# GpSimd normalises the next sequence's rows in place of VectorE, in a gated cross-attention and expert block

## The reference, cut to what matters

```python
def _layernorm(x, axis=-1, eps=1e-05):
    m = jnp.mean(x, axis=axis, keepdims=True)
    v = jnp.var(x, axis=axis, keepdims=True)
    return (x - m) / jnp.sqrt(v + eps)

# attention, 16 heads of 16 columns, causal over the 512 rows, on x = layernorm(x)
q, k, v = heads(x @ Wq + bq), heads(x @ Wk + bk), heads(x @ Wv + bv)
att = where(causal, q k^T / 4, -inf);  y = softmax(att) @ v
y = y + softmax(qc kc^T / 4) @ vc            # the same rows against the context
return y @ Wp + bp

x = x + tanh(g_xattn) * attention(layernorm(x), ctx)
x = x + tanh(g_ffn) * experts(layernorm(x))  # top 2 of 16, and a shared one with a convolution
```

## Times and profile before

| | us |
|---|---|
| median of 3 runs | 1772.03 |
| lowest and highest | 1766.85, 1774.86 |
| the profiled execution | 1767.04 |
| its span, from the first to the last instruction | 1765.3 |
| its mean granted TensorE clock, share of full speed | 0.967 |

### The profile page before, as it was taken

One profiled execution on the slowest core, in us unless ns is written; L12 is line 12 of the kernel. 1 busy time (PEld: TensorE's weight loads), 2 busy tenths in 40 slices (PEclk: granted clock), 3 DMA queues, 4 the chain that ended last, 5 costly groups with the idle time before them and its releaser, 6 DMA issues.

```text
span 1765.3 us, 36714 instructions
## 1 busy us (share of the span) xinstructions
PE 1588.7 (90%) x11515; PEld 958.3 (54%) x11515; DVE 1240.4 (70%) x3358; ACT 841.1 (48%) x1716; POOL 937.2 (53%) x1556
## 2 busy tenths in 40 slices
PE   2499899989999999999999999999975999997997
PEld 1245455545545554555555555555543999984554
DVE  1377677767777777777777777777844776665776
ACT  1156455555556555555655555555441444431111
POOL 3134455635445554544555454455544766647775
PEclk9799999999999999999999999999986999998999
DMA  3443656555544656565355655546444666656886
GB/s 105 133 130 94 136 99 161 95 143 120 138 122 101 163 96 159 110 142 130 93 165 101 151 125 127 136 87 164 95 128 113 183 172 172 171 149 194 258 259 196
DMA packets 215399, 247.95 MB, mean 140 GB/s; under 512 B 51368, under 2 KB 168624, under 8 KB 215216
## 3 DMA queue, kind: packets, MB, share of 16 engines
q1 hardware_dynamic: 177136, 191.06, 44.0%
q0 software_dynamic: 17344, 35.75, 7.9%
q10 hardware_dynamic: 20736, 18.88, 3.1%
HBM read 160.04 MB, written 85.53 MB: 139 GB/s over the span
## 4 chain that ended last, share of the span: by engine, by line
PE 66%; DVE 9%; POOL 7%; issue 6%; DMA 4%; ACT 3%; SPq 1%; DVEq 0%; POOLq 0%; ACTq 0%
PE pv_self L1256 9%; PE scalar_bank L1184 9%; PE scalar_bank L1195 8%; PE vector_bank L1668 7%; POOL pt L1789 6%; PE vector_bank L1230 6%; DVE nmax L1049 4%; PE vector_bank L1227 4%; PE vector_bank L1299 3%; PE vector_bank L1141 3%; PE pv_cross L1239 3%; PE vector_bank L1174 3%; PE pv_cross L1676 2%; PE scalar_bank L1657 2%; PE pv_self L1676 2%
## 5 line engine op out<-in xcount | busy, mean ns | idle before, releaser
L1049 DVE TENSOR_REDUCE nmax<-vector_bank 128x1 f32<-128x384 f32 (+4 forms) x832 | 513.4, 640 | 164.2 <-PE vector_bank L1230 158.1
L752 ACT ACTIVATE pt<-scalar_bank 128x512 f32<-128x512 f32 x640 | 363.2, 598 | 239.9 <-PE scalar_bank L1195 238.1
L615 POOL TENSOR_SCALAR_AFFINE_SELECT pt<-pt 128x256 f32<-128x256 f32 (+1 forms) x640 | 224.4, 366 | 151.1 <-ACT pt L752 142.6
L1195 PE MATMUL scalar_bank<-stack 99*64 99x512 bf16 (+4 forms) x1280 | 294.4, 321 | 3.2 <-DMA stack<-max_scratch 2.2
L627 POOL TENSOR_TENSOR parts<-q,parts 128x1600 bf16<-128x1600 f32 x32 | 103.1, 3222 | 289.1 <-ACT parts L728 289.1
L1230 PE MATMUL vector_bank<-stack 96*128 96x128 bf16 (+3 forms) x1024 | 249.0, 302 | 0.0
L1227 PE MATMUL vector_bank<-tri,ident_b 128*128 128x128 bf16 (+2 forms) x704 | 176.4, 251 | 49.6 <-DVE nmax L1049 17.5
L1184 PE MATMUL scalar_bank<-xnT,w_qk 128*128 128x512 f32 x384 | 194.6, 632 | 1.3 <-ACT xnT L705 1.3
L1227 PEld LDWEIGHTS vector_bank<-tri,ident_b 128*128 128x128 bf16 x704 | 68.5, 97 | 231.3 <-DVE nmax L1049 115.6
L1500 POOL DMA_INDIRECT pt<-xn_rows,idx x144 | 144.2, 1001 | 77.8 <-issue 62.0
L1256 PE MATMUL pv_self<-pt,vst 128*32 128x512 f32 (+3 forms) x2048 | 181.3, 443 | 3.2 <-ACT usum L739 2.0
(11 more groups left out here) (213 smaller groups left out, 2689.2 us busy)
## 6 DMA issues: line engine op xcount, KB each, us to landing
qk_scratch<-parts SPq DMA_DIRECT2D x32, 1200.0 KB
stack<-qk_scratch SPq DMA_DIRECT2D x128, 192.0 KB, 4.3
stack<-qk_scratch SPq DMA_DIRECT2D x256, 72.0 KB, 3.3
results<-pt ACTq DMA_DIRECT2D x144, 128.0 KB
stack<-qk_scratch SPq DMA_DIRECT2D x128, 128.0 KB, 4.1
stack<-qk_scratch SPq DMA_DIRECT2D x256, 36.0 KB, 3.0
xt<-in_x_dram SPq DMA_DIRECT2D x17, 512.0 KB, 4.2
xr<-in_x_dram SPq DMA_DIRECT2D x16, 512.0 KB, 5.0
```

The lines of the kernel that those rows point to most:

```text
L615: pool.affine_select(out=v, in_=v, compare_op=ALU.is_ge, fill=0.0, base=0, pattern=pat, channel_multiplier=-1).then_inc(masked, 1)
L752: act.activation(dst, bank(kind, ("st", c, k))[:, :], ACT.Exp, scale=SCALE).then_inc(scalar_drained, 1)
L1049: dve.tensor_reduce(dst, src, axis=AX, op=ALU.max, negate=True).then_inc(vector_drained, 1)
L1195: return pe.matmul(out, stack[c][0:rows, head, key0:key0 + nk], stack[c][0:rows, head, q0:q0 + nq], start=True, stop=True, **kw)
```

## The change

GpSimd does what `ln_apply` did for every sequence but the very first, whose four tiles stay on VectorE. In the bodies with a current and a next sequence one tile stands in each of the steps 8 to 11 of group (1, 1), ahead of the step's scatter and mask. In the prologue the four tiles stand in a row between `rstd` and `split_max`.

```diff
-LN_ROWS = {(1, 20 + t): t for t in range(4)}
+LN_ROWS = {8 + t: t for t in range(4)}
@@ gpsimd
+            def normalised(kind, b, t):
+
+                if t == 0:
+                    pool.wait_ge(rstd_ready, LN.upto(kind, b, 0) + 1)
+                    pool.wait_ge(scalar_filled, SU.upto(kind, b, ("xT", QT - 1)))
+                last = pool.tensor_scalar(xn[:, t, :], xt[:, t, :], mv[:, t, 0:1], rstd[:, t:t + 1],
+                                          ALU.subtract, ALU.mult)
+                if t == QT - 1:
+                    last.then_inc(xn_ready, 1)
+
             def mask_group(kind, b, c, g):
 
                 for k, name in enumerate(GROUP):
+                    if k in LN_ROWS and (c, g) == (1, 1) and PARTS[kind][2]:
+                        normalised(kind, b, LN_ROWS[k])
...
                 if nxt and not cur:
                     rstd_of(LN.upto(kind, b, 0) + 1)
+                    for t in range(QT):
+                        normalised(kind, b, t)
                     split_max(kind, b, 0, 0)
@@ vector, beside
-                    if (c, k) in LN_ROWS:
-                        if LN_ROWS[c, k] == 0:
-
-                            dve.wait_ge(scalar_filled, SU.upto(kind, b, ("xT", QT - 1)))
-                        ln_apply(n, LN_ROWS[c, k])
```

## The result

The changed kernel took 1843.47 us in the median of 4 runs (1836.64 to 1848.0), the kernel before 1770.33 beside it on the same chip: ratio 1.0408, 95% interval 1.0367 to 1.045. It is 73 us slower; 14 were forecast (1785.9), and 1843 lies outside the range of 1771 to 1803. The profiled execution took 1848.0 us, its span 1846.3; it is the longest of the four, as the profiled one before (1767.04) is near the shortest of its own, so that the two traces lie 81 us apart and not 73.

A forecast was written before the change was run, and what follows sets the result against it. TensorE was taken to bound the kernel, with GpSimd's masks already holding its products; 14 x 0.90 = 12.6 us plus 1.3 in the prologue gave 13.9, on the 1772.03 median 1785.9 us, range 1771 to 1803.

The forecast's parts named there:

- the price of the tile: One normalising tile on GpSimd, called c, was taken at 0.45 us, with ends of 0.40 and 0.82.
- The dearest value that I allowed: A GpSimd tile at twice VectorE's 486 ns, 0.97 us, giving 43.7 us of loss and 1815.7; chance 0.03.
- The rule of the queue: Last head group: products end later by the largest of 2c, 3c - 0.5 and 4c - 1.0, 0.90 us a sequence.
- A3: Mask of head 3's first key tile, last head group; two tiles ahead delay it 2c, forecast as deciding, 0.90 us.
- prologue 4.9 - 0.5: Prologue: TensorE gets the split maxima 4c later, forecast 1.8 us, less 0.5 given back by VectorE; net 1.3 us.
- The first sequence, counted at 0: Sequence without scatters: mask A3 has 2.0 us in hand and its masks wait for ScalarE, so no loss, 0.
- The freed VectorE: VectorE's freed 1.94 us a sequence counted as nothing; the rival that it wins gave 1756.8 us, chance 0.05.
- GpSimd takes up its lag before the additions into y: After the masks, GpSimd's extra lag of 4c fits in its 1.92 us idle before the additions, less TensorE's own 0.9.
- GpSimd is dearer: Rival: a tile costs 0.72 to 0.82 us and the last mask decides, 29 to 35 us lost; chance 0.16 overall.
- the marks that the text set for being wrong: Steady sequence near 76 us, idle at the products over 1.5 us, or low stretches in over ten or under four sequences.
- more of the low clock: Rival: all 14 steady sequences get a low-clock stretch, six more costing 10 us, 1796 us; chance 0.16.
- VectorE's tile beside it had stretched the mask B3 by 0.1 us: Last head group: this mask took 0.51 us where 0.40 is usual; without VectorE's overlap 0.1 us comes back.

The follow-up runs named there:

- forms: Changed kernel with each of the four GpSimd tiles in another form (one or two steps, column scalars or immediates); 1915.51 us against 1864.45 before, ratio 1.0282.
- copy4: Changed kernel with each GpSimd tile a plain copy of x in the same place; 1878.0 us against 1864.45 for the kernel before, ratio 1.0084.
- late1: Changed kernel with each GpSimd tile one mask later, the fourth behind all masks; 1898.46 us against 1859.32 for the kernel before, ratio 1.0216.
- moved: Changed kernel with the last head group's two scatters behind its last mask; 1789.82 us against 1761.66 for the kernel before, ratio 1.0164.
- after2: The changed kernel again, unaltered, on another chip; 1828.08 us against 1761.66 for the kernel before, ratio 1.0378.
- prologue: Changed kernel with only the prologue's four tiles on GpSimd, VectorE normalising in all bodies; 1862.74 us against 1859.32 for the kernel before, ratio 1.0024.
- free: Kernel before, VectorE leaving out the steady sequences' tiles but keeping their waits and signal, GpSimd untouched; 1757.7 us against 1761.66, ratio 0.9979.
- none: Changed kernel without the GpSimd tiles, their two waits left on GpSimd; 1872.58 us against 1864.45 for the kernel before, ratio 1.0041.
- before2: The kernel before once more, unchanged, for differences between chips; 1857.36 us against 1859.32, ratio 0.9998.

## Why the prediction was wrong

**The step that failed is the price of the tile**: "With the fixed part of the opcode and the slope of the one-input operation, 0.233 + 252 x 0.000875 = 0.45 us." It measured 1.22 us. A slope was carried from one opcode (the mask) to another because both read one tensor. forms and copy4 show that the number of inputs doesn't set it: with one input each, tensor_scalar took 848 to 1235 ns and the copy 395. The dearest value that I allowed, twice VectorE's time, 0.97 us, was still too low: the ratio to VectorE's mean of 486 ns is 2.5, and to its median of 414 it is 3.0. With that, also the weighing of ends failed: the row of the same opcode bounded only its fixed part, and no row bounded its slope from above.

The Trainium skill, "GPSIMD Engine Reference", section 4.1, has a one-input operation on GpSimd at about line rate. The copy fits that (395 ns, where VectorE's copies of this size, out of PSUM, took 412 to 417 in the kernel before), and the mask (409 ns) is near it; the normalising (1224 ns) and its plainest form (848 ns) do not fit. The opening of the page, VectorE roughly 2x faster, pointed the right way and is still short of 2.5. The measurement decides.

**The rule of the queue held.** Put c = 1.22 into the largest of 2c, 3c - 0.5 and 4c - 1.0: 3.88 us, where the trace has 3.93 to 4.04. forms (3.09 against 3.18), late1 (2.67 against 2.67) and copy4 (0.79 against 0.8) hold it at three other points, and moved comes near (1.4 against 1.2). The last mask decides and not A3, as the prediction said it would at 0.72 us.

**The sum again with c = 1.22**: 14 x 3.88 = 54.3, prologue 4.9 - 0.5 = 4.4, together 58.7 us, against 13.9. This accounts for 45 of the some 58 us by which the forecast was short. The two traces are 81 us apart: 6.3 in the prologue, 2.8 in the first sequence, 64.8 in the thirteen steady ones read whole (13 x 3.93 = 51 of them) and 6.9 behind the last rstd, where the fourteenth late products lie. What the rest is:

- The first sequence, counted at 0, is not free. With tiles of 1.22 us its masks are late too: the same 0.42 and 0.50 us of idle time inside its products, 0.4 (after2) to 2.8 us on the whole.
- The prologue took 5.4 to 6.3 us more rather than 4.4, in the change's two profiles, 3.9 with prologue alone. TensorE at 1.2 GHz behind the longer idle time is what the difference shows (3.78 us against 2.05 or 2.84 for the same 16 products).
- Low-clock stretches, and waits ahead of L1236. In the profiled execution each of the thirteen has at least one low-clock stretch, six had none before. Many fall in the slowed products and cost little there (80.4 to 80.9 us, against 80.0 in after2 for a sequence with none). But two sequences took 88.7 and 88.4 us, with the clock at 0.94:

```profile
245.30:334.00 88.70, 78.68 (x584) 42.09 (x585) 59.16 (x162) 44.86 (x87) 45.56 (x82) 0.94 0.48 115
```

```profile
556.67 0.58 PE L1236 MATMUL vector_bank<-tri,ident_b 128*128 128x512 bf16 x1 [4.87 <-issue]
```

  In both TensorE idles 3.8 to 4.9 us ahead of L1236 and runs slowly behind it. Over the 81.6 us of the others that is some 14 of the 81 us between the two profiled executions. after2 has this less, and is 67 us slower rather than 73. Waits of that kind stand in the kernel before as well (4.09 us at 366, where the line is L1227), and the profile names nothing that ends them. Beyond thirteen times its full-clock sequence the steady part takes 20 us before, 32 after and 17 in after2, so whether the change brings any of this or the execution does is not settled; the two intervals, 1.0367 to 1.045 and 1.035 to 1.0406, overlap.

**The other steps.** The freed VectorE was counted at nothing and gave nothing (free, and 3.93 us more idle time ahead of the sums). That GpSimd takes up its lag before the additions into y holds: the sequence grew by the products' lateness and no more. The rival "GpSimd is dearer" was the right one, with its price set too low (29 to 35 us, at the dearest 43.7). Of the marks that the text set for being wrong, two came true: idle time at the products above 1.5 us (2.74, and 3.66 with the two short ones), and more than ten sequences with a low stretch (thirteen of thirteen, and eleven in after2, against seven before). The rival "more of the low clock" had the count nearly right, but not as the cause: the time beyond full clock grew by 12 of the steady part's 65 us in this execution, and not at all in after2. That VectorE's tile beside it had stretched the mask B3 by 0.1 us holds: it took 0.51 us and 0.40 in the trace after.

## What to carry to other kernels

The slope of an instruction belongs to its opcode and its engine: where the trace has the opcode only over 4 elements, its time over 256 is unknown, and the range has to say so rather than borrow the slope of another opcode. Before work is moved to an engine that looks half idle, count what stands between its last free moment and the first consumer on the bounding engine; here the four tiles in front of the last mask cost their full length, less 1 us of slack, in all 14 sequences, and moving two scatters out of that queue more than halved the loss (29 us in place of 67). The same queue pointed the other way to a faster kernel: small work that nobody waits for, standing ahead of masks that TensorE waits for.

## What the runs showed of the hardware

- GpSimd's tensor_scalar over 128x256 fp32 takes 848 ns with one step and an immediate, 924 with one step and a column, 1078 with two steps and immediates, 1224 to 1235 with two steps and columns; copy 395, mask 409, tensor_tensor add 724. In the prologue, with VectorE idle, the full form takes the same 1.22 us.
- Two semaphore waits already met, ahead of an indirect DMA on GpSimd, raised the gap ahead of it from 0.19 to 0.58 us (none), and that stood on the path: 0.40 us in 11 of the 13 sequences read.
- TensorE's products in pieces that each wait cost more than the waits: 0.42 + 0.50 us of idle time inside, and 2.78 us for the pieces (1.07 + 1.07 + 0.64) in place of 2.36 for the block, with ends that the profile models.
- The same program with the same instructions showed one wait as 0.69 us on one chip and, in most sequences, as 1.02 us on another, and waits of 1.3 us at the products in three of thirteen sequences of one execution (before2) that another on the same chip (prologue) did not have. A difference of a few tenths of a microsecond in a sequence is to be read on the same chip and in like sequences.
